# Order of the first maxima, a lead that shrinks, and GpSimd's order of work, in a kernel of FFN, attention and FFN on one Trainium2 core

## The chip, the cores and the metric

The kernel runs on one core of a Trainium2 chip. The time is device microseconds from launch to end, as a median over several executions; the smaller the better. The core's engines run side by side and each takes its own instructions in order: TensorE (PE), VectorE (DVE), ScalarE (ACT), GpSimd (POOL) and SyncE (SP). They wait for one another through semaphores. SP and POOL issue the DMAs that this text speaks of.

## The reference

For one sequence of 2048 tokens with 128 features:

```python
x = x + 0.5 * ffn(layernorm(x))    # 128 -> 512 (ternary weights), gelu, layernorm, 512 -> 128 (ternary weights)
x = x + attention(layernorm(x))    # 16 heads of 8 features
x = x + 0.5 * ffn(layernorm(x))
# attention, per head: q and k are turned by the rotary tables, then
scores = q @ k.T / sqrt(8)         # 2048 x 2048
attn = softmax(scores, axis=-1)
out = attn @ v                     # then all heads together @ wo.T + bo
```

The softmax is taken with the maximum of each row of scores subtracted. The scores are so large that this subtraction is needed, and it has to be the maximum over all 2048 keys.

## The kernel before

There are 8 pairs of heads and 4 chunks of 512 queries, so 32 **groups** (one pair, one chunk of queries; `NG`), taken chunk by chunk. Every group is worked on twice.

**First pass, the maxima.** A group has 16 **max units** (`A_STEP`): 4 key chunks of 512 keys (`kb`) times 4 tiles of 128 queries (`q`). In a unit PE multiplies queries with keys for the two heads of the pair (`max_mm`, L1307, two matmuls of 128x512 into two PSUM banks; there are two such pairs of banks) and DVE takes the maximum over the keys (`row_max`, L819, 128x1024 in, 128x2 out). A max matmul of unit n waits until DVE has done unit n - 2 (`a_free`). There are 512 units in all. One unit after a group's last, DVE joins the four key chunks' maxima (`whole_max`, L827); GpSimd splits the result into three bf16 parts in five small operations (`cut_max`, L526 to L530); two units further on DVE transposes the parts (`max_rows`, L836), for which it waits for GpSimd (`mp_ready`); then SP and POOL send them with four DMAs each (`rows`, L353 and L538) into three extra rows of the queries in `QT`. The second pass's product then gives the score less the maximum, with no further work.

**Second pass, the exponentials.** A group has 16 **exp units**. In one, PE multiplies keys with queries, for the two heads (`exp_mm`, L1326, two matmuls of 128x512, in three PSUM banks in turn), ACT takes the exponential of each (`exp_tile`, L1082), and PE multiplies the result with the values, two units behind (`pv_tile`, L1339, eight matmul records on 128x256). In the third exp of the next group ACT copies the group's sums out of PSUM (`take_out`, L1090), and SP and POOL send them on with four DMAs each (`sums`, L364 and L549).

**The coupling.** PE's list is written out by hand. First come 25 max units (`LEAD`), the last eight of them with a matmul that serves only to keep PE at work (`warm`, L1137). From there on every step holds one exp unit, one max unit that is 25 ahead, and one `pv_tile`. The first exp matmul of a group waits for the group's eight row DMAs (`m_in`). After exp unit 487 there are no max units left; work of the last layers is put among the last exp units (`late`).

**The start of the maxima.** They begin while the keys and queries are still being laid out. For each of the key chunks K0 to K3 and for the first query chunk Q0, DVE and ACT cut the turned values into three bf16 parts (on DVE `rest`, L747, and `last_part`, L754; on ACT `first_cut`, L1009, and `second_cut`, L1015). PE then places them by one-hot matmuls (`place_half`, L1226, six matmuls) and ACT copies them out of PSUM (`put`, L1031 and L1034), in four steps for each: parity 0 or 1 of the pair number, half 0 or 1. Group 0 needs parity 0, group 1 parity 1. In DVE's list the last cuts of K2 and K3 stand behind max units 1, 2, 4 and 5; DVE's last one of K3 waits for ACT's `second_cut("K3")`. PE's list has the placings between the first max units.

**GpSimd's list.** In round i: `sums(i - 1)`, `cut_max(i + 1)`, `rows(i + 1)`, then pieces of the later query chunks. SP has the same order without the cut.

Of the kernel before, what the change touches and what calls it, by code (L numbers as in the profile page):

```python
# [9 lines left out]
ALU = mybir.AluOpType  # L10
# [33 lines left out]
B_STEP = 2 * NT  # L44
QH = CS // 2
PV_LAG = 2
LEAD = 25
PRING = 16
NG = NC * PAIRS
UNITS = NG * A_STEP  # L50
# [4 lines left out]
OUT_AT = 2  # L55
ROW_DMAS = 4
OD_DMAS = 4

WIDE_FROM = (2 * (UNITS - LEAD) + 3) // 4 * 4
WIDE = 5  # L60
# [7 lines left out]

QK_SEQ = ("K0", "Q0", "K1", "K2", "K3")
UNIT_SEQ = ("K0", "Q0", "K1", "Q1", "K2", "Q2", "K3", "Q3")  # L70
PLACE_SEQ = (("K0", 0), ("Q0", 0), ("K1", 0), ("K0", 1), ("Q0", 1), ("K2", 0), ("K1", 1), ("K3", 0), ("K2", 1), ("K3", 1))
UNIT_BANKS = 3
PARTS = 3
VB = 3
# [21 lines left out]
def macaron(nc, x, wq, bq, wk, bk, wv, bv, wo, bo, w_fc, ln_w, ln_b, w_proj, out):  # L96
# [4 lines left out]
    with ExitStack() as ctx:  # L101
# [234 lines left out]
        @block.sync  # L336
        def _(sp):
            tokens = x.rearrange("a (t p) d -> p (a t) d", p=P)
            sp.dma_start(wfc_n[:, :, :], w_fc.rearrange("(k p) d -> p k d", p=P)).then_inc(wf_in, 16)
            sp.dma_start(X[:, 0:CT, :], tokens[:, 0:CT, :]).then_inc(x0_in, 16)  # L340
            sp.dma_start(wpj_n[:, :], w_proj).then_inc(wp_in, 16)
            sp.dma_start(X[:, CT:NT, :], tokens[:, CT:NT, :]).then_inc(x_in, 16)
            sp.wait_ge(x_in, 16)
            sp.wait_ge(w_in, 16 * W_DMAS)
            for n in range(2):
                sp.dma_start(rope[:, n, :], rope_dram[:, n, :]).then_inc(rope_in, 16)

            def rows(g):

                j, c = g % PAIRS, g // PAIRS  # L350
                sp.wait_ge(rows_ready, g + 1)
                for a in range(4):
                    sp.dma_start(row_slots(0, j, c, a), mrow[32 * a:32 * a + 3 * CT, g % 2, :])\  # L353
                        .then_inc(m_in[0][j], 16)

            def sums(g):

                sp.wait_ge(po_free, g + C_ONE + 1)
                if g >= 2 * PAIRS and g % PAIRS == 0:
                    sp.wait_ge(ot_ready, g // PAIRS - 1)  # L360
                for kind in range(2):
                    for half in range(2):
                        to, at = sum_rows(0, kind, half, g)
                        sp.dma_start(to, at).then_inc(o_out[0][g % 2], 16)  # L364

            def spread(c):

                sp.wait_ge(od_rec, c + 1)
                sp.dma_start(recip_dram[c], dense[:, c % 2, :]).then_inc(rec_out, 16)
                sp.wait_ge(rec_out, 16 * (c + 1))  # L370
                whole = recip_dram[c].rearrange("(g s) n -> g (s n)", s=HD)
                sp.dma_start(OD[:, c % 2, 1, :], whole.unsqueeze(1).broadcast_to([NH, HD, CS])).then_inc(rec_in, 16)

            def q_bounce(c):

                sp.wait_ge(q_step, 7 * c)
                sp.dma_start(q_dram[c - 1], q_cut[:, :, :]).then_inc(q_out, 16)

            def q_scatter(c, first):

                sp.wait_ge(q_out, 16 * c)
                for r in range(first, first + Q_DMAS // 2):
                    to, at = q_slots(0, c, r)
                    sp.dma_start(to, at).then_inc(q_in[0][c - 1], 16)

            rows(0)
            for g in range(NG):
                if g:
                    sums(g - 1)
                if g + 1 < NG:  # L390
                    rows(g + 1)
                if g > PAIRS and g % PAIRS == 3:
                    spread(g // PAIRS - 1)
                c = g // Q_STEPS
                if 1 <= c < NC:
                    if g % Q_STEPS == 0:
                        q_bounce(c)
                    else:
                        q_scatter(c, Q_DMAS // 2 * (g % Q_STEPS - 1))
            sums(NG - 1)  # L400

            for c in range(NC):

                sp.wait_ge(y_ready, c + 1)
                sp.dma_start(out.rearrange("a (t p) d -> p (a t) d", p=P)[:, c * CT:(c + 1) * CT, :],
                             chunk(Y, c)).then_inc(y_out, 16)
            sp.wait_ge(y_out, 16 * NC)
# [3 lines left out]
        def _(pool):  # L411
# [149 lines left out]
            for i in range(NG):  # L561
                if i == NG - 1:
                    for c in range(NC - 1):
                        ln_scale(2, c, c)
                if i:
                    sums(i - 1)
                if i + 1 < NG:
                    cut_max(i + 1)
                    rows(i + 1)
                if i > PAIRS and i % PAIRS == 4:  # L570
                    divide(i // PAIRS - 1)
                c = i // Q_STEPS
                if c + 1 < NC:
                    q_piece(c + 1, i % Q_STEPS)
                if 1 <= c < NC and i % Q_STEPS:
                    q_scatter(c, Q_DMAS // 2 * (i % Q_STEPS - 1))
                if i < NC:
                    bias_rows(i)
# [13 lines left out]
        def _(dve):  # L592
# [219 lines left out]

            def row_max(n):

                u = n % A_STEP
                q, kb = u % CT, u // CT
                bank = A0 + 2 * (n % 2)
                dve.wait_ge(a_ready, n + 1)
                v.tensor_reduce(mh[:, n // A_STEP % 2, :, q, kb], ps[:, bank:bank + 2, :], AX.X, ALU.max)\  # L819
                    .then_inc(a_free, 1)  # L820

            def whole_max(i):

                dve.wait_ge(a_free, (i + 1) * A_STEP)
                if i:
                    dve.wait_ge(mp_ready, i)
                v.tensor_reduce(top[:, :], mh[:, i % 2, :, :, :].rearrange("p h q n -> p (h q) n"), AX.X, ALU.max)\  # L827
                    .then_inc(top_ready, 1)
# [17 lines left out]
            for n in range(UNITS):  # L846
# [6 lines left out]
                    rest("K3")  # L853
                if n == 5:
                    last_part("K3")
                g, u = n // A_STEP, n % A_STEP
                if g and u == TOP_AT - 1:
                    whole_max(g - 1)
                if g and u == CUT_AT - 1:
                    max_rows(g - 1)  # L860
                if g > PAIRS and g % PAIRS == 3 and u == REC_AT:
                    reciprocals(g // PAIRS - 1)
            whole_max(NG - 1)
# [45 lines left out]
        def _(act):  # L909
# [152 lines left out]
            put("Q0", 1, 1)  # L1062
            first_cut("K3")
            second_cut("K2")
            put("K2", 0, 0)
            put("K2", 0, 1)
            put("K1", 1, 0)
            put("K1", 1, 1)
            second_cut("K3")
            put("K3", 0, 0)  # L1070
            put("K3", 0, 1)
            put("K2", 1, 0)
# [32 lines left out]
        def _(pe):  # L1105
# [179 lines left out]
            def max_mm(m):  # L1285

                n, x = m // 2, m % 2
                g, u = n // A_STEP, n % A_STEP
                j, c = g % PAIRS, g // PAIRS
                h, q, kb = 1 - x, u % CT, u // CT  # L1290
                rows = slice(HR * h, HR * h + R_QK)
                if x == 0:
                    if n >= 2:
                        pe.wait_ge(a_free, n - 1)
                    elif n == 0:
                        for last in range(2 * len(UNIT_SEQ) - UNIT_BANKS, 2 * len(UNIT_SEQ)):
                            unit_wait(pe, last)
                        pe.wait_ge(v_free, NC)
                    if g == 0 and q == 0:
                        pe.wait_ge(place_ev, 2 * max(PLACE_SEQ.index((y, 0)) for y in ("Q0", f"K{kb}")) + 1)  # L1300
                    if g == 1 and u == 0:
                        pe.wait_ge(place_ev, 2 * len(PLACE_SEQ))
                    if c and j == 0 and u == 0:
                        for part in range(2):
                            pe.wait_ge(q_in[part][c - 1], 16 * Q_DMAS)
                at = c * CS + q * P
# [58 lines left out]
                    last.then_inc(turned, 1)  # L1365


            for n in range(LEAD):
                max_mm(2 * n)
                max_mm(2 * n + 1)  # L1370
                if n == 1:
# [4 lines left out]
                if n == 3:  # L1376
                    place_half("Q0", 1, 1)
                if n == 5:
                    place_half("K2", 0, 0)
                    place_half("K2", 0, 1)  # L1380
                if n == 6:
                    place_half("K1", 1, 0)
                if n == 7:
                    place_half("K1", 1, 1)
                if n == 9:
                    place_half("K3", 0, 0)
                    place_half("K3", 0, 1)
                if n == 10:
                    place_half("K2", 1, 0)
                if n == 11:  # L1390
                    place_half("K2", 1, 1)
                if n == 12:
                    place_half("K3", 1, 0)
                if n == 13:
                    place_half("K3", 1, 1)
                if n > A_STEP:
                    warm(1, EXP[1])
            for g in range(NG):
                for k in range(B_STEP):
                    n = g * B_STEP + k  # L1400
                    exp_mm(g, k)
                    if k % 2 and n + 2 * LEAD < 2 * UNITS:
                        max_mm(n - 1 + 2 * LEAD)
                        max_mm(n + 2 * LEAD)
                    if n < WIDE_FROM:
                        if k % 2 and n // 2 >= PV_LAG:
                            pv_tile(n // 2 - PV_LAG)
# [57 lines left out]
```

## Time and profile before

| | us |
|---|---|
| median of 3 runs | 767.67 (766.25 to 768.15) |
| the profiled execution's own time | 763.32 |
| its span, first to last instruction | 761.4 |
| of that: before the first max unit on DVE | 84.0 |
| first exp matmul on PE | 128.4 |
| last max unit on DVE ends | 688.9 |
| last exponential on ACT ends | 715.9 |

The profile shows one execution. An engine's busy time is the time in which an instruction of it runs; PE's matmuls are pipelined, so a PE that is shown busy need not be at its peak. The times of single instructions are counted from the start of the span. The 2 us between span and time lie outside the instructions.

### The profile page before, as it was taken

The numbers are of one execution on the slowest core, as the hardware profiler recorded it, in microseconds if no ns is written. First come the engines' busy times: TensorE is split into PE (matmuls) and PEld (weight loads), VectorE is DVE, ScalarE is ACT, GpSimd is POOL, SyncE is SP. The second block draws the span as 40 slices with busy tenths as digits, with TensorE's granted clock in tenths as the row PEclk, the third lists the DMA queues.
The fourth block names the chain that finished last, engine by engine and source line by source line (L and its number), as shares of the span: only waits on it lengthen the run. The fifth ranks groups of instructions, "written<-read, shape, count | busy, mean of one in ns | idle before, by whom it ended". The sixth has DMA issues, their size and how long they took to land.

```text
span 761.4 us, 17532 instructions
## 1 busy us (share of the span) xinstructions
PE 722.2 (95%) x6843; PEld 242.9 (32%) x6843; DVE 688.8 (90%) x880; ACT 637.3 (84%) x1196; POOL 256.9 (34%) x526
## 2 busy tenths in 40 slices
PE   5898779999999999999999999999999999999994
PEld 2774211222222222222222222222222222224373
DVE  6678659999999999999999999999999999996374
ACT  3544643999999999999999999999999999999842
POOL 4332001455455445233323332232222222424321
PEclk8999755999999999999999999999999999999998
DMA  7000000000011011011000000000000000000001
GB/s 221 2 1 0 1 0 2 3 5 4 24 25 25 24 25 25 25 24 40 4 4 4 4 4 3 5 19 5 4 4 4 5 6 21 7 7 3 7 15 42
DMA packets 22674, 12.45 MB, mean 16 GB/s; under 512 B 13088, under 2 KB 21152, under 8 KB 22336
## 3 DMA queue, kind: packets, MB, share of 16 engines
q1 hardware_dynamic: 11328, 8.77, 4.1%
q0 software_dynamic: 9056, 2.04, 1.6%
q8 instruction: 54, 0.88, 0.5%
q10 hardware_dynamic: 2208, 0.53, 0.4%
q14 instruction: 28, 0.23, 0.1%
HBM read 7.34 MB, written 2.33 MB: 13 GB/s over the span
## 4 chain that ended last, share of the span: by engine, by line
DVE 63%; PE 28%; issue 4%; ACT 2%; DMA 1%; POOL 0%; SPq 0%; DVEq 0%; POOLq 0%; ACTq 0%
DVE mh L819 59%; PE ps L1339 7%; PE ps L1326 5%; PE ps L1126 3%; PE ps L1307 3%; PE ps L1226 2%; PE ps L1185 2%; PE ps L1202 2%; ACT KT L1031 1%; DVE ring L681 1%; PE ps L1354 1%; DMA X<-in_L_attn_x_dram 1%; DMA QT<-mrow 0%; PE ps L1192 0%; DVE mrow L836 0%
## 5 line engine op out<-in xcount | busy, mean ns | idle before, releaser
L819 DVE TENSOR_REDUCE mh<-ps 128x2 f32<-128x1024 f32 x512 | 584.8, 1213 | 6.3 <-PE ps L1307 6.2
L1082 ACT ACTIVATE ring<-ps 128x512 f32<-128x512 f32 x1024 | 551.2, 600 | 30.6 <-PE ps L1326 15.9
L1339 PE MATMUL ps<-ring,Vx 128*32 128x256 f32 x4096 | 325.4, 392 | 0.9 <-ACT outT L1090 0.9
L1307 PE MATMUL ps<-KT,QT 48*128 48x512 bf16 x1024 | 209.3, 392 | 10.1 <-DVE mh L819 9.7
L1326 PE MATMUL ps<-QT,KT 51*128 51x512 bf16 x1024 | 212.6, 388 | 1.7 <-DMA QT<-mrow 0.6
L1339 PEld LDWEIGHTS ps<-ring,Vx 128*32 128x32 f32 x4096 | 82.0, 108 | 172.0 <-ACT ring L1082 156.4
L1326 PEld LDWEIGHTS ps<-QT,KT 51*128 51x128 bf16 x1024 | 51.9, 93 | 220.6 <-ACT ring L1082 205.6
L549 POOL DMA_DIRECT2D rope<-outT x80 | 42.9, 542 | 147.4 <-ACT outT L1090 139.6
L538 POOL DMA_DIRECT2D QT<-mrow x128 | 71.7, 565 | 42.2 <-DVE mrow L836 38.7
L526 POOL TENSOR_TENSOR mp<-zeros,top 128x8 bf16<-128x8 f32 x32 | 6.3, 198 | 223.3 <-DVE top L827 223.3
L1307 PEld LDWEIGHTS ps<-KT,QT 48*128 48x128 bf16 x1024 | 50.1, 94 | 52.4 <-DVE mh L819 23.8
L959 ACT ACTIVATE ring<-ps 128x512 f32<-128x512 f32 x32 | 18.0, 601 | 26.2 <-PE ps L1126 14.3
L1126 PE MATMUL ps<-QT,WfcT 128*128 128x512 f32 x64 | 32.8, 651 | 2.0 <-ACT QT L946 1.4
L1185 PE MATMUL ps<-WpC,ring 128*128 128x129 f32 x256 | 30.4, 276 | 1.5 <-ACT ring L959 1.5
L1185 PEld LDWEIGHTS ps<-WpC,ring 128*128 128x128 f32 x256 | 29.4, 191 | 2.5 <-ACT ring L959 1.6
L1031 ACT ACTIVATE KT<-ps,k_ones 128x1024 bf16<-128x1024 f32 x16 | 17.4, 1111 | 14.4 <-PE ps L1226 14.3
L549 POOL DMA_DIRECT2D dense<-outT x48 | 24.0, 505 | 1.0 <-issue 0.9
L681 DVE TENSOR_TENSOR ring<-ring 128x512 f32<-128x512 f32 x24 | 18.8, 784 | 1.2
L1090 ACT COPY outT<-ps 128x256 f32<-128x256 f32 x32 | 12.0, 374 | 9.3 <-PE ps L1339 9.3
L457 POOL TENSOR_TENSOR rsh<-var,half_neg 128x4 f32<-128x4 f32 x8 | 9.3, 1161 | 28.5 <-DVE var L703 28.5
L965 ACT ACTIVATE ring<-ring 128x512 f32<-128x512 f32 x32 | 17.6, 636 | 0.0
L1202 PE MATMUL ps<-ring,WQK 128*128 128x512 f32 x32 | 17.3, 661 | 0.1
(133 smaller groups left out, 344.0 us busy)
## 6 DMA issues: line engine op xcount, KB each, us to landing
rope<-rope_tables SPq DMA_DIRECT2D x2, 1024.0 KB, 6.2
QT<-mrow SPq DMA_DIRECT2D x128, 0.8 KB
QT<-mrow POOLq DMA_DIRECT2D x128, 0.8 KB, 1.7
rope<-outT SPq DMA_DIRECT2D x80, 8.0 KB
rope<-outT POOLq DMA_DIRECT2D x80, 8.0 KB, 1.7
q_bounce<-XB SPq DMA_DIRECT2D x3, 384.0 KB, 2.4
QT<-q_bounce SPq DMA_DIRECT2D x18, 64.0 KB
QT<-q_bounce POOLq DMA_DIRECT2D x18, 64.0 KB, 3.2
```

The lines of the kernel that those rows point to most:

```text
L538: g.dma_start(row_slots(1, j, c, a), mrow[32 * a + 3 * CT:32 * a + 6 * CT, i % 2, :])\
L549: g.dma_start(to, at).then_inc(o_out[1][i % 2], 16)
L681: last = v.tensor_tensor(sqsum[:, n % 2, :], sqsum[:, n % 2, :] if k > 1 else sq[:, 0, :], sq[:, k, :], ALU.add)
L819: v.tensor_reduce(mh[:, n // A_STEP % 2, :, q, kb], ps[:, bank:bank + 2, :], AX.X, ALU.max)\
L1031: a.activation(KT[:, first:first + 3:2, c * CS:(c + 1) * CS], at, ACT.Identity, bias=k_ones[:, 3:4])\
L1082: a.activation(ring[:, n % PRING, :], ps[:, exp_bank(n), :], ACT.Exp, scale=SCALE).then_inc(p_ready, 1)
L1126: t.matmul(ps[:, FC + k, :], WfcT[:, k * P:(k + 1) * P], XF[:, c * CS:(c + 1) * CS], start=True, stop=True).then_inc(fc_ready, 1)
L1185: last = t.matmul(out_tile(i, n % 2)[:, 0:D + 1], hid[:, k, i * P:(i + 1) * P], WpC[:, k, :], start=(k == 0), stop=(k == KH - 1))
L1202: t.matmul(ps[:, u % UNIT_BANKS, :], WQK[:, n, k, :], XT[:, c % 2, :], start=True, stop=True)\
L1307: mm = t.matmul(ps[:, A0 + 2 * (n % 2) + h, :], QT[rows, j, at:at + P], KT[rows, j, kb * CS:(kb + 1) * CS], start=True, stop=True)
L1326: t.matmul(ps[:, exp_bank(n), :], KT[rows, j, kt * P:(kt + 1) * P], QT[rows, j, c * CS:(c + 1) * CS], start=True, stop=True).then_inc(b_re ...
L1339: mm = t.matmul(ps[r:r + 32, PO, 0:QH], Vx[:, kt, col:col + 32], ring[:, (2 * n + h) % PRING, half * QH:(half + 1) * QH], start=(kt == 0), ...
```

## The change

1. **Order of the maxima.** The 32 max units of groups 0 and 1 are done together, by key chunk: chunk 0 of both groups, chunk 1 of both, chunks 2 and 3 of group 0, chunks 2 and 3 of group 1 (`TURNS`, `ORDER`). Group 0 then ends with unit 23 instead of 15, group 1 with unit 31 as before (`LAST_OF`); `whole_max` and `max_rows` follow one and three units behind. The waits for the placings are per key chunk in group 1 too.
2. **Order of the placings.** K1's parity 1 comes before K2's parity 0 in PE's and ACT's lists, ACT's `second_cut("K3")` comes two `put`s earlier, and no two halves are placed right behind each other from K1 parity 1 on.
3. **Lead.** 34 max units stand ahead of the first exp unit instead of 25 (six of them with a `warm` instead of eight). At exp units 47, 95, ..., 431 the max unit is left out, so that the lead falls by one each time, to 25.
4. **GpSimd's and SP's order.** In rounds 0 to 10 `cut_max(i + 1)` and `rows(i + 1)` stand ahead of `sums(i - 1)`; from round 11 on as before.

```diff
+LEAD_FIRST = 34
 LEAD = 25
+LEAD_STEP = 48
+CUTS_FIRST = 11
...
+TURNS = ((0, 0), (1, 0), (0, 1), (1, 1), (0, 2), (0, 3), (1, 2), (1, 3))
+ORDER = [(g, q, kb) for g, kb in TURNS for q in range(CT)]
+ORDER += [(g, u % CT, u // CT) for g in range(2, NG) for u in range(A_STEP)]
+LAST_OF = [max(n for n, (of, _, _) in enumerate(ORDER) if of == g) for g in range(NG)]
...
-PLACE_SEQ = (("K0", 0), ("Q0", 0), ("K1", 0), ("K0", 1), ("Q0", 1), ("K2", 0), ("K1", 1), ("K3", 0), ("K2", 1), ("K3", 1))
+PLACE_SEQ = (("K0", 0), ("Q0", 0), ("K1", 0), ("K0", 1), ("Q0", 1), ("K1", 1), ("K2", 0), ("K3", 0), ("K2", 1), ("K3", 1))
...
             for g in range(NG):
+                if g < CUTS_FIRST:
+                    rows(g + 1)
                 if g:
                     sums(g - 1)
-                if g + 1 < NG:
+                if CUTS_FIRST <= g < NG - 1:
                     rows(g + 1)
...
+                if i < CUTS_FIRST:
+                    cut_max(i + 1)
+                    rows(i + 1)
                 if i:
                     sums(i - 1)
-                if i + 1 < NG:
+                if CUTS_FIRST <= i < NG - 1:
                     cut_max(i + 1)
                     rows(i + 1)
...
+                if n - TOP_AT in LAST_OF:
+                    whole_max(LAST_OF.index(n - TOP_AT))
+                if n - CUT_AT in LAST_OF:
+                    max_rows(LAST_OF.index(n - CUT_AT))
                 g, u = n // A_STEP, n % A_STEP
-                if g and u == TOP_AT - 1:
-                    whole_max(g - 1)
-                if g and u == CUT_AT - 1:
-                    max_rows(g - 1)
...
             second_cut("K2")
-            put("K2", 0, 0)
-            put("K2", 0, 1)
             put("K1", 1, 0)
             put("K1", 1, 1)
             second_cut("K3")
+            put("K2", 0, 0)
+            put("K2", 0, 1)
...
-                    if g == 0 and q == 0:
-                        pe.wait_ge(place_ev, 2 * max(PLACE_SEQ.index((y, 0)) for y in ("Q0", f"K{kb}")) + 1)
-                    if g == 1 and u == 0:
+                    if g < 2 and q == 0:
+                        pe.wait_ge(place_ev, 2 * max(PLACE_SEQ.index((y, g)) for y in ("Q0", f"K{kb}")) + 1)
+                    if g == 2 and q == 0 and kb == 0:
                         pe.wait_ge(place_ev, 2 * len(PLACE_SEQ))
...
-            for n in range(LEAD):
+            for n in range(LEAD_FIRST):
                 max_mm(2 * n)
                 max_mm(2 * n + 1)
...
                 if n == 5:
+                    place_half("K1", 1, 0)
+                if n == 6:
+                    place_half("K1", 1, 1)
+                if n == 8:
                     place_half("K2", 0, 0)
+                if n == 9:
                     place_half("K2", 0, 1)
-                if n == 6:
-                    place_half("K1", 1, 0)
-                if n == 7:
-                    place_half("K1", 1, 1)
-                if n == 9:
+                if n == 11:
                     place_half("K3", 0, 0)
+                if n == 12:
                     place_half("K3", 0, 1)
-                if n == 10:
+                if n == 14:
                     place_half("K2", 1, 0)
-                if n == 11:
+                if n == 15:
                     place_half("K2", 1, 1)
-                if n == 12:
+                if n == 17:
                     place_half("K3", 1, 0)
-                if n == 13:
+                if n == 18:
                     place_half("K3", 1, 1)
-                if n > A_STEP:
+                if n > 27:
                     warm(1, EXP[1])
+            lead = LEAD_FIRST
             for g in range(NG):
                 for k in range(B_STEP):
                     n = g * B_STEP + k
                     exp_mm(g, k)
-                    if k % 2 and n + 2 * LEAD < 2 * UNITS:
-                        max_mm(n - 1 + 2 * LEAD)
-                        max_mm(n + 2 * LEAD)
+                    if k % 2 and lead > LEAD and n // 2 % LEAD_STEP == LEAD_STEP - 1:
+                        lead -= 1
+                    elif k % 2 and n + 2 * lead < 2 * UNITS:
+                        max_mm(n - 1 + 2 * lead)
+                        max_mm(n + 2 * lead)
```

## Rows read from the trace of the kernel before

**Rows 1.** Chain that ended last, shares by line.
```profile
DVE mh L819 59%; PE ps L1339 7%; PE ps L1326 5%; PE ps L1126 3%; PE ps L1307 3%; PE ps L1226 2%; PE ps L1185 2%; PE ps L1202 2%; ACT KT L1031 1%; DVE ring L681 1%; PE ps L1354 1%; DMA X<-in_L_attn_x_dram 1%; DMA QT<-mrow 0%; PE ps L1192 0%; DVE mrow L836 0%
```
**Rows 2.** Stretches: busy us and instructions of PE, PEld, DVE, ACT, POOL; clock; DMA.
```profile
205.03:223.32 18.29, 18.26 (x194) 5.10 (x192) 18.29 (x20) 17.54 (x34) 9.53 (x18) 1.00 0.12 25
...
131.20:134.60 3.40, 3.40 (x24) 0.54 (x22) 2.80 (x3) 1.94 (x4) 0.00 (x0) 0.50 0.00 0
134.60:138.00 3.40, 3.40 (x42) 0.89 (x40) 3.08 (x4) 2.93 (x6) 0.00 (x0) 1.00 0.02 5
```
**Rows 3.** Timeline of ACT, copies of groups' sums: start, us, instruction, idle before.
```profile
150.25 0.37 ACT L1090 COPY outT<-ps 128x256 f32<-128x256 f32 x1 [0.22 <-PE ps L1339]
...
186.75 0.37 ACT L1090 COPY outT<-ps 128x256 f32<-128x256 f32 x1 [0.24 <-PE ps L1339]
205.03 0.37 ACT L1090 COPY outT<-ps 128x256 f32<-128x256 f32 x1 [0.24 <-PE ps L1339]
...
627.19 0.37 ACT L1090 COPY outT<-ps 128x256 f32<-128x256 f32 x1 [0.24 <-PE ps L1339]
```
**Rows 4.** Timeline of DVE, 14 max units of a group in a row.
```profile
142.26 15.89 DVE L819 TENSOR_REDUCE mh<-ps 128x2 f32<-128x1024 f32 x14
```
**Rows 5.** Timeline of PE, exp pairs from 336 to 355 us, behind a stall.
```profile
336.54 0.39 PE L1326 MATMUL ps<-QT,KT 51*128 51x512 bf16 x2
...
353.19 0.81 PE L1326 MATMUL ps<-QT,KT 51*128 51x512 bf16 x2
354.72 0.39 PE L1326 MATMUL ps<-QT,KT 51*128 51x512 bf16 x2
```
**Rows 6.** Timeline of DVE and of PE, what lengthened single groups.
```profile
311.31 0.54 DVE L844 RECIPROCAL dense<-dense 128x64 f32<-128x64 f32 x1
...
331.66 0.39 PE L1326 MATMUL ps<-QT,KT 51*128 51x512 bf16 x2 [0.57 <-DMA QT<-mrow]
```
**Rows 7.** Timeline of PE, the last step with a max unit and the first without.
```profile
686.79 0.39 PE L1326 MATMUL ps<-QT,KT 51*128 51x512 bf16 x2
...
687.89 0.39 PE L1326 MATMUL ps<-QT,KT 51*128 51x512 bf16 x2
...
688.79 1.06 PE L1326 MATMUL ps<-QT,KT 51*128 51x512 bf16 x4
```
**Rows 8.** Timeline of DVE, last cut of K3, max units 19 to 27, 29 to 32.
```profile
102.61 0.69 DVE L754 TENSOR_TENSOR XB<-X,XB 128x512 bf16<-128x512 f32 x1 [5.59 <-ACT XB L1015]
...
122.66 10.44 DVE L819 TENSOR_REDUCE mh<-ps 128x2 f32<-128x1024 f32 x9
...
135.25 4.62 DVE L819 TENSOR_REDUCE mh<-ps 128x2 f32<-128x1024 f32 x4 [0.33 <-PE ps L1307]
```
**Rows 9.** Timeline of ACT, copies of placed keys and the second cut of K3.
```profile
96.26 2.12 ACT L1031 ACTIVATE KT<-ps,k_ones 128x1024 bf16<-128x1024 f32 x2 [3.96 <-PE ps L1226]
...
101.97 0.61 ACT L1015 CAST XB<-X 128x512 bf16<-128x512 f32 x1
```
**Rows 10.** Timeline of PE, placings, and the first exp units.
```profile
94.76 1.48 PE L1226 MATMUL ps<-early,place 32*128 32x512 bf16 x12
...
97.52 1.46 PE L1226 MATMUL ps<-XB,place 32*128 32x512 bf16 x6 [0.74 <-ACT KT L1031]
...
127.29 0.61 PE L1307 MATMUL ps<-KT,QT 48*128 48x512 bf16 x2
...
128.37 0.61 PE L1326 MATMUL ps<-QT,KT 51*128 51x512 bf16 x2
...
132.62 0.61 PE L1326 MATMUL ps<-QT,KT 51*128 51x512 bf16 x2
...
134.60 0.39 PE L1326 MATMUL ps<-QT,KT 51*128 51x512 bf16 x2
```
**Rows 11.** Timeline of POOL, the sums' DMAs and the cut of one group.
```profile
187.41 1.07 POOL L549 DMA_DIRECT2D rope<-outT  x2 [1.21 <-ACT outT L1090]
...
194.89 0.20 POOL L526 TENSOR_TENSOR mp<-zeros,top 128x8 bf16<-128x8 f32 x1 [5.41 <-DVE top L827]
```

More of the change, by code:

```diff
@@ L813, in row_max @@
             def row_max(n):
-                u = n % A_STEP
-                q, kb = u % CT, u // CT
+                g, q, kb = ORDER[n]
                 bank = A0 + 2 * (n % 2)
                 dve.wait_ge(a_ready, n + 1)
-                v.tensor_reduce(mh[:, n // A_STEP % 2, :, q, kb], ps[:, bank:bank + 2, :], AX.X, ALU.max)\
+                v.tensor_reduce(mh[:, g % 2, :, q, kb], ps[:, bank:bank + 2, :], AX.X, ALU.max)\
                     .then_inc(a_free, 1)
             def whole_max(i):
-                dve.wait_ge(a_free, (i + 1) * A_STEP)
+                dve.wait_ge(a_free, LAST_OF[i] + 1)
                 if i:
@@ L1287, in max_mm @@
                 n, x = m // 2, m % 2
-                g, u = n // A_STEP, n % A_STEP
+                g, q, kb = ORDER[n]
                 j, c = g % PAIRS, g // PAIRS
-                h, q, kb = 1 - x, u % CT, u // CT
+                h = 1 - x
                 rows = slice(HR * h, HR * h + R_QK)
@@ L1298, in max_mm @@
                         pe.wait_ge(v_free, NC)
-                    if g == 0 and q == 0:
-                        pe.wait_ge(place_ev, 2 * max(PLACE_SEQ.index((y, 0)) for y in ("Q0", f"K{kb}")) + 1)
-                    if g == 1 and u == 0:
+                    if g < 2 and q == 0:
+                        pe.wait_ge(place_ev, 2 * max(PLACE_SEQ.index((y, g)) for y in ("Q0", f"K{kb}")) + 1)
+                    if g == 2 and q == 0 and kb == 0:
                         pe.wait_ge(place_ev, 2 * len(PLACE_SEQ))
-                    if c and j == 0 and u == 0:
+                    if c and j == 0 and q == 0 and kb == 0:
                         for part in range(2):
```

## The prediction

> **What bounds the kernel now.** I read the chain of waits first: DVE's maxima are 59% of it, PE's value and exp matmuls 12% [rows 1]. The table of stretches comes next. In one group of the steady middle DVE is busy for 18.29 of 18.29 us, PE for 18.26, ACT for 17.54 at overlapping instructions, and the clock is 1.00 [rows 2]. So two engines could be the bound, and which one it is decides the change. The timelines tell them apart.
>
> DVE: 14 max units take 15.89 us, so one starts every (15.89 - 1.22) / 13 = 1.13 us; 16 of them and 0.2 for a group's top and transpose are 18.28, which is the distance of two copies of sums, 186.75 to 205.03 [rows 3, 4]. DVE paces that group. PE: behind a stall it runs free for a whole group. Its exp pairs go from 336.54 to 354.72, 18.18 us for 16 steps; 15 steps are 1.11 and one, at the group's seam, 353.19 to 354.72, is 1.53, since ACT copies the sums there [rows 5]. So PE needs 18.18 a group and DVE 18.28: **PE is only 0.10 us a group away from being the bound itself.** ACT isn't one: its step is that of PE in both cases, with room in PE's waits at the seam alone.
>
> The sum is made against the profiled execution: 763.32 us, of which 761.4 are the span. The median of the runs is 767.67, 4.3 above it; I add the difference that I find to the median.
>
> **Part 1 and 2: the first 34 max units.** Before, DVE stood idle 5.59 us ahead of the last cut of K3 [rows 8], since ACT reached its second cut of K3 only at 101.97, behind four `put`s, two of which waited for placings [rows 9]. In the new order two of them remain ahead of it. K1's parity 1 is placed at 94.76 (a half takes 1.46 busy and 1.41 to the next, from 97.52 [rows 10]), the second half behind the next max pair at 96.7, its copy ends at 99.3, the cut of K3 follows and ends at 99.9. DVE's last cut starts there, 2.7 us before 102.61. Nothing ahead of it moves: max unit 4 is of group 1 now and needs Q0's parity 1, whose copy stands ahead of all this on ACT.
>
> From there I walked the two lists. DVE needs 1.13 for a unit. PE needs, at the low clock, 0.54 for a max pair (127.29 to 127.83 is one, then a filler of the same length up to the exp pair at 128.37 [rows 10]) and 1.41 for a placing, so 1.95 for a unit that has one. Eight units from 8 to 18 have one, where before two placings, those of K2 and K3 at parity 0, ran as a pair: 12 matmuls in 1.48 [rows 10]. With three units to 0.54 x 3 + 1.41 x 2 = 4.4 PE against 3.4 on DVE, DVE is short by about 1 us per three units while placings last. Unit 6 starts at 100.5, unit 9 at 104.4, unit 12 at 108.8, unit 15 at 113.2, unit 18 at 117.6, unit 19 at 119.6. Unit 19 started at 122.66 before [rows 8]. So the order gains **3.1 us** on DVE at unit 19, of which 2.7 is the cut. Then DVE runs on without a gap, where before it was PE with its fillers that set 1.15 a unit (10.44 for nine) and the slow first exp units: unit 31 ends at 119.6 + 12 x 1.13 + 0.3 (top and transpose of group 0) + 1.2 less the overlap of 0.1 = 134.6, and unit 32 ends at 135.7 against 139.87 before (135.25 + 4.62 [rows 8]): 4.2 us earlier.
>
> The Trainium skill has a rule that speaks against this part: in "TensorE: Matmul & The Clock Gate", section "Why this matters for your kernels", matmuls of few rows that use distinct groups of rows run at the same time. By it the two halves of a placing, which use different rows, cost one half's time when they stand together, and the new order, which pulls K2's and K3's apart, pays 2 x 1.41 = 2.8 us more on PE; priced by the count of matmuls it would pay nothing. The trace agrees with the rule (12 in 1.48 beside 6 in 1.46 [rows 10]).
>
> **Part 3: the lead.** The first exp pair comes behind 34 max units. The last of these is issued when DVE has done unit 31, at 134.6; a pair and a filler later (1.08, as 127.29 to 128.37) the exp pair starts at 135.7. Before it was 128.37 [rows 10]. **The exponentials start 7.3 us later.** Group 0's rows are no hindrance: its transpose is at about 128.7, 7.0 ahead of the exp pair, where before there were 5.8. What the exp units then save:
> - A step without a max pair takes 0.90 (687.89 to 688.79) instead of 1.10 (686.79 to 687.89) [rows 7]. Nine of them save 9 x 0.2 = 1.8.
> - With 47 max units to 48 exp units DVE needs 3 x 18.28 - 1.13 = 53.7, PE 3 x 18.18 - 0.2 = 54.3. So PE becomes the bound and DVE gets idle time of 0.6 in every step of the lead. From the first sums' copy to that of group 26 there were 26 groups in 627.19 - 150.25 = 476.9 [rows 3]. At PE's pace they are 26 x 18.18 = 472.7, less 1.8: 470.9. That saves **6.0 us**. It contains three stalls of 0.4, where DVE's reciprocals (0.54, the first at 311.31) broke its pace, and one of 0.57, where an exp pair waited for rows behind other DMAs at 331.66 [rows 6]; an idle DVE and earlier rows hide them.
> - After exp unit 432 the lead is 25 again, and everything to the end is as before.
>
> The sum: 7.3 - 6.0 = **+1.3 us**. The 6.2 us from the first exp pair to the high clock (128.37 to 134.60 [rows 2, 10]) are taken to be as long as before. The profiled execution would be 764.6, the median 769.0.
>
> Bounds: PE's pace can't be above DVE's 18.28 without being the old kernel's; were it 18.28 in free running too, 2.6 of the 6.0 would be gone: +3.9. If PE could be left out and DVE alone set the end, the 4.2 us of max unit 32 are the other bound: -4.2.
>
> **Part 4: GpSimd's order.** With a lead of 34 the top of group i + 1 comes at exp unit 16i or so, two units before the sums' copy. The five operations (0.20 each from 194.89, 0.28 apart) take 1.3, the four DMAs of sums 2 x 1.07 [rows 11]. Behind these, the parts would be late by about 3 us and DVE's transpose would wait; the new order avoids that, so it costs nothing and gains nothing against before, where the top came seven units behind. What is queued behind the two waits on POOL (for the top, for the transpose) are the sums' DMAs, the pieces of later queries and, on SP, its own sums: up to 5 us later, while the copy that needs their buffer is a group off. In round 11, with lead 31, the cut stands behind the sums again, with 2.2 us until the transpose; it can be late by 0.3, which DVE's new idle time takes up. If that cover is gone it is 0.3, once.
>
> **The rivals.**
> - *DVE is the bound all the way.* Then the end follows DVE: 4.2 earlier, less what DVE loses in the slow first exp units as before (0.60 in 131.20 to 134.60, 0.32 in the next 3.4 us [rows 2]), so -3.3: 764.4. For it: DVE is the engine that is busy for the full 18.29 and has 59% of the chain. Against it: PE's free group of 18.18.
> - *The clock stays low longer, and the kernel gets slower.* Its place is the start of the exp units. A step takes 1.98 (132.62 to 134.60) at clock 0.50 and 1.11 after it [rows 2, 5, 10], so each us more at the low clock costs 0.44. PE is less dense than before from 119.6 to 129, since the fillers there are gone. With 3.2 us more the price is 1.4: +2.6, 770.3. It decides from 2.5 us more on. Against it: before, too, the clock stayed low throughout the fillers and rose only when value matmuls ran.
> - *The cut of K3 is not earlier*, because the halves of K1 wait or PE holds ACT up. Then the change doesn't do what part 2 says; the exponentials start 2.7 later still: +3.9, 771.6.
>
> **How the numbers follow.** From no change this kernel's measurement can tell about 0.3%, 2.3 us. Forecast +1.3: 0.50, its own range -1.0 to +3.5, of which same 0.39, slower 0.10, faster 0.01. DVE bound: 0.22, of which faster 0.19, same 0.03. Low clock: 0.15, slower 0.09, same 0.06. Late cut: 0.13, slower 0.11, same 0.02. Together faster 0.20, same 0.50, slower 0.30. The range goes from DVE's bound, less 0.5 (763.9), to late cut plus some of the low clock (+4.6, 772.3).
>
> **What would show it.** DVE's last cut of K3 at 99.9 and max unit 32 ending near 135.7; the first exp pair at 135.7; sums' copies 18.1 apart (three groups 54.3) up to group 26 and 18.28 after it; DVE idle by 0.2 a group, waiting for max matmuls; no wait for rows. It is wrong if the copies stay at 18.28 while the lead falls (then +3.9), if DVE has no idle time but groups are shorter than 18.1, or if the first exp pair is off by more than 1.5 us.

## The result and the profile after

The changed kernel is **slower: ratio 1.0048, 95% interval 1.0038 to 1.0058**. Its median is 768.53 us (767.79 to 771.97, 20 runs) against 764.98 us (763.30 to 768.15, 20 runs) for the kernel before, so +3.6 us. The forecast was +1.3, with 0.50 for "no change" and 0.30 for "slower"; the time lies in the range, the move lies outside what I called no change (2.3 us). That the forecast time, 769.0, and the measured 768.53 agree within 0.5 us is luck: the forecast stood on a median of 767.67 over three runs of the kernel before, and over 20 runs it is 764.98.

The two profiled executions differ by more, 770.26 and 763.32, because the first is high and the second low in what its kernel scatters. So I compare stretches that start at an event of the kernel: the first max unit on DVE, the first exp pair on PE, the copies of the sums on ACT.

| us | before | before, second profile | after | after with cut order 14 |
|---|---|---|---|---|
| first max unit to max unit 19 | 38.65 | 37.79 | 33.86 | 35.11 |
| first max unit to first exp pair | 44.36 | 43.50 | 49.98 | 51.23 |
| first exp pair to first copy of sums | 21.89 | 22.75 | 22.88 | 21.89 |
| first copy to copy of group 26 | 476.94 | 477.00 | 474.57 | 473.95 |
| copy of group 26 to copy of group 31 | 90.75 | 90.75 | 90.60 | 90.60 |
| copy of group 31 to the end | 43.45 | 45.08 | 45.09 | 43.45 |

(The second and the fourth column are experiments told below; the fourth is the same code as the third up to round 11. The start of the exp units and the stretches at the low clock scatter by 1 to 2 us from execution to execution, so two profiles of each are shown.) Between the means of two columns each: the exp units start 6.7 later, the 26 groups give back 2.7 (2.4 in the changed kernel itself), the rest 0.15. That is +3.8 to +4.1, beside +3.6 measured.

The chain of waits has moved from DVE to PE (shares of the span by line; L832 is the maximum, L1352 the values, L1339 the exp pairs, L1320 the max pairs). Beside it stands [rows 1].

```profile
PE 78%; DVE 15%; issue 3%; ACT 2%; POOL 1%; DMA 1%; DVEq 0%; POOLq 0%; SPq 0%; ACTq 0%
PE ps L1352 32%; PE ps L1339 20%; PE ps L1320 13%; DVE mh L832 11%; PE ps L1139 3%; PE ps L1198 2%; PE ps L1239 2%; PE ps L1215 1%; ACT KT L1044 1%; DVE ring L695 1%; PE ps L1367 1%; DMA X<-in_L_attn_x_dram 1%; PE ps L1205 0%; PE ps L1225 0%; DVE X L727 0%
```

The timeline of ACT after, the copies of the sums (start, us, instruction, idle before), beside [rows 3]. Groups are 18.18 apart where they were 18.28; 176.39 to 194.53, which holds a step without a max pair, is 18.14, only 0.04 less; and 340.26 to 359.11 is 18.85.

```profile
158.21 0.37 ACT L1103 COPY outT<-ps 128x256 f32<-128x256 f32 x1 [0.22 <-PE ps L1352]
176.39 0.37 ACT L1103 COPY outT<-ps 128x256 f32<-128x256 f32 x1 [0.22 <-PE ps L1352]
194.53 0.37 ACT L1103 COPY outT<-ps 128x256 f32<-128x256 f32 x1 [0.22 <-PE ps L1352]
212.71 0.37 ACT L1103 COPY outT<-ps 128x256 f32<-128x256 f32 x1 [0.22 <-PE ps L1352]
...
340.26 0.37 ACT L1103 COPY outT<-ps 128x256 f32<-128x256 f32 x1 [0.24 <-PE ps L1352]
359.11 0.37 ACT L1103 COPY outT<-ps 128x256 f32<-128x256 f32 x1 [0.22 <-PE ps L1352]
...
632.78 0.37 ACT L1103 COPY outT<-ps 128x256 f32<-128x256 f32 x1 [0.22 <-PE ps L1352]
```

The table of stretches after (busy us and instructions of PE, PEld, DVE, ACT, POOL; clock; DMA), beside [rows 2]: a group without a short step, and the last stretch at the low clock with the next one.

```profile
212.71:230.89 18.18, 18.15 (x194) 4.61 (x192) 18.18 (x19) 17.54 (x33) 9.53 (x18) 1.00 0.16 26
140.40:143.82 3.42, 3.42 (x24) 0.67 (x24) 2.41 (x2) 1.98 (x4) 3.42 (x3) 0.50 0.03 6
143.82:147.24 3.42, 3.42 (x40) 0.82 (x36) 2.97 (x4) 3.11 (x6) 0.18 (x1) 1.00 0.00 0
```

The timeline of DVE after, the first maxima, beside [rows 8]. The last cut of K3 (L768) starts at 99.92, and DVE then waits 0.71 for a max pair at every third unit.

```profile
99.92 0.69 DVE L768 TENSOR_TENSOR XB<-X,XB 128x512 bf16<-128x512 f32 x1 [2.82 <-ACT XB L1028]
...
114.91 3.59 DVE L832 TENSOR_REDUCE mh<-ps 128x2 f32<-128x1024 f32 x3 [0.71 <-PE ps L1320]
119.20 6.88 DVE L832 TENSOR_REDUCE mh<-ps 128x2 f32<-128x1024 f32 x6 [0.71 <-PE ps L1320]
```

The timeline of PE after, a step without a max pair (a **short step**; it starts at 191.11), beside [rows 7]. It takes 0.89. The next takes 1.29. All nine such places show these two numbers. DVE then waits for its max pair (third fence; the second has the two ACT exponentials that the reading of the banks below rests on).

```profile
191.11 0.39 PE L1339 MATMUL ps<-QT,KT 51*128 51x512 bf16 x2
...
192.00 0.57 PE L1339 MATMUL ps<-QT,KT 51*128 51x512 bf16 x2
...
193.29 0.39 PE L1339 MATMUL ps<-QT,KT 51*128 51x512 bf16 x2
...
194.40 0.39 PE L1339 MATMUL ps<-QT,KT 51*128 51x512 bf16 x2
```
```profile
190.42 0.60 ACT L1095 ACTIVATE ring<-ps 128x512 f32<-128x512 f32 x1
...
191.53 0.60 ACT L1095 ACTIVATE ring<-ps 128x512 f32<-128x512 f32 x1
```
```profile
192.83 2.36 DVE L832 TENSOR_REDUCE mh<-ps 128x2 f32<-128x1024 f32 x2 [0.47 <-PE ps L1320]
```

### The profile page after: what moved, and what is told of

Same layout as the page of the kernel before. It is cut to its first block, busy times and chain, and to the rows that moved or that the text cites. A ratio compares the mean times of both kernels' runs of the same rounds, so it can differ in the third digit from the quotient of the medians.

```text
span 768.5 us, 17532 instructions
## 1 busy us (share of the span) xinstructions
PE 729.2 (95%) x6841; PEld 243.1 (32%) x6841; DVE 690.6 (90%) x880; ACT 636.4 (83%) x1196; POOL 256.9 (33%) x526
## 4 chain that ended last, share of the span: by engine, by line
PE 78%; DVE 15%; issue 3%; ACT 2%; POOL 1%; DMA 1%; DVEq 0%; POOLq 0%; SPq 0%; ACTq 0%
PE ps L1352 32%; PE ps L1339 20%; PE ps L1320 13%; DVE mh L832 11%; PE ps L1139 3%; PE ps L1198 2%; PE ps L1239 2%; PE ps L1215 1%; ACT KT L1044 1%; DVE ring L695 1%; PE ps L1367 1%; DMA X<-in_L_attn_x_dram 1%; PE ps L1205 0%; PE ps L1225 0%; DVE X L727 0%
## 5 line engine op out<-in xcount | busy, mean ns | idle before, releaser
L832 DVE TENSOR_REDUCE mh<-ps 128x2 f32<-128x1024 f32 x512 | 586.2, 1211 | 12.0 <-PE ps L1320 11.9
L1352 PE MATMUL ps<-ring,Vx 128*32 128x256 f32 x4096 | 325.9, 392 | 0.9 <-ACT outT L1103 0.9
L1320 PE MATMUL ps<-KT,QT 48*128 48x512 bf16 x1024 | 211.4, 395 | 12.6 <-DVE mh L832 12.4
L1339 PE MATMUL ps<-QT,KT 51*128 51x512 bf16 x1024 | 214.8, 389 | 1.1
L1352 PEld LDWEIGHTS ps<-ring,Vx 128*32 128x32 f32 x4096 | 82.3, 108 | 187.7 <-ACT ring L1095 167.0
L1339 PEld LDWEIGHTS ps<-QT,KT 51*128 51x128 bf16 x1024 | 52.9, 93 | 221.0 <-ACT ring L1095 205.7
L1320 PEld LDWEIGHTS ps<-KT,QT 48*128 48x128 bf16 x1024 | 50.3, 95 | 44.5 <-DVE mh L832 29.7
L1198 PE MATMUL ps<-WpC,ring 128*128 128x129 f32 x256 | 33.6, 294 | 1.5 <-ACT ring L972 1.5
L1198 PEld LDWEIGHTS ps<-WpC,ring 128*128 128x128 f32 x256 | 32.6, 209 | 2.5 <-ACT ring L972 1.6
L457 POOL TENSOR_TENSOR ve<-mv,eps 128x4 f32<-128x4 f32 x12 | 3.2, 264 | 41.6 <-DVE mv L617 41.6
```

Source lines behind the costliest of these rows:

```text
L832: v.tensor_reduce(mh[:, g % 2, :, q, kb], ps[:, bank:bank + 2, :], AX.X, ALU.max)\
L1198: last = t.matmul(out_tile(i, n % 2)[:, 0:D + 1], hid[:, k, i * P:(i + 1) * P], WpC[:, k, :], start=(k == 0), stop=(k == KH - 1))
L1320: mm = t.matmul(ps[:, A0 + 2 * (n % 2) + h, :], QT[rows, j, at:at + P], KT[rows, j, kb * CS:(kb + 1) * CS], start=True, stop=True)
L1339: t.matmul(ps[:, exp_bank(n), :], KT[rows, j, kt * P:(kt + 1) * P], QT[rows, j, c * CS:(c + 1) * CS], start=True, stop=True).then_inc(b_re ...
L1352: mm = t.matmul(ps[r:r + 32, PO, 0:QH], Vx[:, kt, col:col + 32], ring[:, (2 * n + h) % PRING, half * QH:(half + 1) * QH], start=(kt == 0), ...
```

## The experiments

The theory: a unit of lead costs one DVE step at the start; in return, while the lead falls, a group takes 18.18 instead of 18.28 us. The rivals: the orders of maxima and placings are what costs; or PE's own work sets the 18.18, and then a step without a max pair is worth 0.2 us (called P in the expectations); or the loop between PE and ACT over three exp banks sets it, and such a step is worth nothing (L).

**The lead alone.** The orders of the changed kernel are set back:

```diff
-TURNS = ((0, 0), (1, 0), (0, 1), (1, 1), (0, 2), (0, 3), (1, 2), (1, 3))
+TURNS = ((0, 0), (0, 1), (0, 2), (0, 3), (1, 0), (1, 1), (1, 2), (1, 3))
...  (PLACE_SEQ, ACT's puts and PE's placings as in the kernel before)
```

> Parts 3 and 4 without parts 1 and 2: orders of maxima and placings as before, first lead 34, nine steps down to 25, GpSimd's order as changed. The first exp pair comes nine DVE steps later than before, 44.4 + 10.3 = 54.7 us behind the first max unit; the groups then save 2.4 us between the first sums' copy and that of group 26, as in the changed kernel. In all +7.5 to +8 us on the kernel before, 1.010; the orders are then worth 4 to 4.5 us of the changed kernel. Rival: the orders themselves are what costs (placings pulled apart), so that this kernel is no slower than the changed one, 1.005.

Ratio 1.0106 (1.0084 to 1.0128, median 774.15). The first exp pair comes 54.07 behind the first max unit (54.7 expected), and the 26 groups take 474.61, as expected. The rival falls: the orders are worth 1.0106 - 1.0048, some 4.4 us of gain (by the two intervals, 2.6 to 6.3), and the lead costs more than they bring.

**A lead of 31.**

```diff
-LEAD_FIRST = 34
+LEAD_FIRST = 31
...
-                    if g == 2 and q == 0 and kb == 0:
+                    if g == 1 and q == 0 and kb == 3:
                         pe.wait_ge(place_ev, 2 * len(PLACE_SEQ))
```

> The changed kernel with a first lead of 31 instead of 34 (six steps down to 25 instead of nine). Both theories price a unit of lead at the start at 1.13 us (DVE's step), so the first exp pair comes 3.4 us earlier than with 34. Theory L (a loop over the three exp banks sets 1.108 us a step, a step without a max pair saves nothing): nine groups fewer run at 18.18 instead of 18.28, +0.9, so -2.5 against the changed kernel, about 1.0015 of the kernel before. Theory P (PE's own work sets the step, each step without a max pair saves 0.2): +1.5, so -1.9, 1.0023 of the kernel before. If the first group's rows come too late for it, the first exp pair waits for a DMA and the gain is under 1.5.

Ratio 1.0031 (1.0017 to 1.0044), so 0.0017 or 1.3 us less than with 34, at the edge of what the two intervals tell apart. By its middle the gain is smaller than both theories said and fits the third case of the expectation. The timeline of PE shows why: the first exp pair waits for the first group's rows.

```profile
133.18 0.61 PE L1339 MATMUL ps<-QT,KT 51*128 51x512 bf16 x2 [0.80 <-DMA QT<-mrow]
```

It stands 48.74 behind the first max unit, against 49.98 and 51.23 with 34. Since group 0 ends at unit 23 and its rows are already awaited here, I take it that a lead under 31 would start the exp units no earlier in this order; no run shows it, and the new orders with the old lead of 25 were not run either. The 26 groups take 474.41, no more than the 474.57 of lead 34. The nine further groups at 18.18 bought nothing, because their 0.9 stands against two things: the wait in round 11 (below) is missing here, and one of DVE's reciprocals began 1.0 us ahead of a short step and was taken up by it (18.18 for its group; with lead 34 it began 4.8 us ahead, and its group took 18.58). L and P are not told apart by this run.

**Half of the value matmuls' columns.** This kernel leaves most keys out of half of the sums and divides the exponent by 64; its output is not the reference's.

```diff
-                        mm = t.matmul(ps[r:r + 32, PO, 0:QH], Vx[:, kt, col:col + 32],
-                                      ring[:, (2 * n + h) % PRING, half * QH:(half + 1) * QH],
+                        part = QH if kt == 0 else QH // 2
+                        mm = t.matmul(ps[r:r + 32, PO, 0:part], Vx[:, kt, col:col + 32],
+                                      ring[:, (2 * n + h) % PRING, half * QH:half * QH + part],
...  (and scale=SCALE / 64 in ACT's exponential)
```

> The changed kernel with the value matmuls at half their columns (128 instead of 256) for all key tiles but the first of a group, so that half of the sums leave out most keys, and with the exponent divided by 64, so that no sum becomes zero; all other work, all waits and all sizes of ACT and DVE stay. It takes some 0.25 us of PE's work out of each step. Theory P: PE is no bound any more, steps behind a seam take under 1.0 us and three groups take DVE's 53.7 us instead of 54.5, in all at least 7 us less. Theory L: steps behind a seam stay at 1.10 to 1.11 us and three groups at 54.2 to 54.5; under 3 us less between the first copy of sums and that of group 26.

The timeline of ACT of this kernel: 272.13 to 290.42 is 18.29, then 17.83, and with the 17.89 from 254.24 three groups take 54.0.

```profile
254.24 0.37 ACT L1103 COPY outT<-ps 128x256 f32<-128x256 f32 x1
272.13 0.37 ACT L1103 COPY outT<-ps 128x256 f32<-128x256 f32 x1 [0.24 <-PE ps L1353]
290.42 0.37 ACT L1103 COPY outT<-ps 128x256 f32<-128x256 f32 x1 [0.25 <-PE ps L1353]
308.25 0.37 ACT L1103 COPY outT<-ps 128x256 f32<-128x256 f32 x1
```

Of three groups one is DVE's 18.28 again, and the two around the short step are 0.4 shorter each. DVE sets them: in these three groups it waits 0.2 us, once. Behind the seam (the step in which ACT copies the sums) that follows a short step, two or three steps take 0.98 or 0.99 us, where L said 1.10 to 1.11, and three groups take less than L's 54.2. L falls, and PE's work is what holds a full group at 18.18. P's size isn't reached either: 54.0 instead of 53.7, and the 26 groups take 470.5, 4.1 less than 474.57, where P said 7 and L under 3; 0.8 of the difference was lost in the first of them (18.96), which began at the low clock.

PE's timeline at a short step of this kernel: the step is 0.21 shorter than in the changed kernel (0.68), and the next takes 1.29 all the same, as its second exp matmul waits 0.4 us for ACT. PE's weight loads (PEld) and ACT show that wait:

```profile
197.24 0.39 PE L1339 MATMUL ps<-QT,KT 51*128 51x512 bf16 x2
...
197.92 0.78 PE L1339 MATMUL ps<-QT,KT 51*128 51x512 bf16 x2
...
199.21 0.47 PE L1339 MATMUL ps<-QT,KT 51*128 51x512 bf16 x2
```
```profile
197.67 0.60 ACT L1095 ACTIVATE ring<-ps 128x512 f32<-128x512 f32 x1
```
```profile
198.31 0.09 PEld L1339 LDWEIGHTS ps<-QT,KT 51*128 51x128 bf16 x1 [0.30 <-ACT ring L1095]
```

The time of the whole tells nothing (ratio 1.000, 0.9975 to 1.0025): in the profiled execution the clock stayed at 1.2 GHz until 167.6, and the first copy came 27.7 behind the first exp pair instead of 22.9. Two of the other executions took 760 us, at a mean granted clock of 0.95 instead of the 0.94 of this one (766.65).

**Sums first in all rounds (part 4 undone).**

```diff
-CUTS_FIRST = 11
+CUTS_FIRST = 0
```

> The changed kernel with part 4 undone (the sums' DMAs ahead of the cut in all rounds, on POOL and SP). The cut has to wait for the sums' copy, which comes about two steps after the top while the lead is 34, then for four DMAs (2.1 us): DVE's transpose waits about 3 us a group at first and less as the lead falls, and the whole falls behind by 15 to 30 us. Rival: DVE's lead over ACT takes it up, and the time stays within 2 us of the changed kernel.

Ratio 1.0523 (1.0499 to 1.0547), 804.76. The 26 groups take 511.18, 36.6 more; copies are up to 24.7 apart. DVE and POOL at one group: the sums' DMAs, then the cut, and DVE's transpose behind it.

```profile
207.21 1.07 POOL L560 DMA_DIRECT2D rope<-outT  x2 [13.37 <-ACT outT L1103]
208.27 1.00 POOL L560 DMA_DIRECT2D dense<-outT  x2
209.28 0.22 POOL L537 TENSOR_TENSOR mp<-zeros,top 128x8 bf16<-128x8 f32 x1
```
```profile
210.65 0.21 DVE L849 STREAM_TRANSPOSE mrow<-mp 128x32 bf16<-128x32 bf16 x1 [3.44 <-POOL mp L541]
```

DVE waits for the cut in 11 groups, 4.3 us in the first two, 3.4 in the third, which the fences show, and less as the lead falls, down to 0.6: 26.3 us in all. That is about what was expected and the rival (within 2 us) falls; that the whole lost more than 30 us was not. A DVE that stands still lets PE run dry, and the clock fell to 1.2 GHz six times between 162 and 306 us. The first of them (PE's wait, then the stretch, columns as above):

```profile
163.04 0.61 PE L1320 MATMUL ps<-KT,QT 48*128 48x512 bf16 x2 [3.70 <-DVE mh L832]
```
```profile
162.30:169.10 6.80, 6.06 (x38) 1.10 (x38) 5.40 (x5) 2.17 (x4) 5.82 (x7) 0.50 0.02 1
```

How the 10 us beyond DVE's waits divide between the low clock and PE's refilling was not measured.

**GpSimd's order up to round 13.**

```diff
-CUTS_FIRST = 11
+CUTS_FIRST = 14
```

> The changed kernel with GpSimd's new order up to round 13 instead of 10. In round 11 the sums stood ahead of the cut and DVE's transpose waited 0.58 us for it; this wait goes, and the distance of the sums' copies of groups 10 and 11 falls from 18.85 to 18.2, with nothing given back later: 0.6 us less between the first copy and that of group 26 (474.0). Rival: the lost time comes from the query chunk's DMAs in the same round, and the distance stays.

One execution, as expected. In the changed kernel DVE's transpose of round 11 waits for the cut (first fence, the timeline of DVE after); here copies of groups 10 and 11 are 18.18 apart (second fence), and the 26 groups take 473.95, 0.62 less.

```profile
344.38 0.21 DVE L849 STREAM_TRANSPOSE mrow<-mp 128x32 bf16<-128x32 bf16 x1 [0.58 <-POOL mp L541]
```
```profile
339.75 0.37 ACT L1103 COPY outT<-ps 128x256 f32<-128x256 f32 x1 [0.25 <-PE ps L1352]
357.93 0.37 ACT L1103 COPY outT<-ps 128x256 f32<-128x256 f32 x1 [0.22 <-PE ps L1352]
```

**The kernel before once more.**

> The kernel before once more, unchanged, for a second profile of it. The groups keep 18.28 and the first exp pair stays 44.4 us behind the first max unit; the start of the first max unit (84.0 in the first profile, 84.4 to 85.4 in five others) and the stretches at the low clock near the end vary from execution to execution. Rival: the first max unit always starts at 84.0 in this kernel, and the later start belongs to the change.

One execution. The first max unit starts at 85.28, the groups take 18.28, and the first exp pair comes 43.5 behind the first max unit (0.9 less than expected). The late start of the maxima belongs to neither kernel.

```profile
85.28 2.36 DVE L819 TENSOR_REDUCE mh<-ps 128x2 f32<-128x1024 f32 x2 [0.97 <-PE ps L1307]
```

**The early cut of K3, in the kernel before.** In the changed kernel the gain at the start came with the lead's cost. This asks for the gain alone.

```diff
             second_cut("K2")
+            second_cut("K3")
             put("K2", 0, 0)
             put("K2", 0, 1)
             put("K1", 1, 0)
             put("K1", 1, 1)
-            second_cut("K3")
```

> The kernel before with one line moved: ACT's second cut of K3 ahead of the four copies of K2 and K1, all else as before. DVE's last cut of K3 starts at about 97 instead of 102.6; PE's placings then pace units 6 to 13 at 1.95 us each, so unit 14 starts at about 112 instead of 116.8 and the first exp pair at about 123.5 instead of 128.4. As DVE paces the groups at 18.28 from there, the whole gain stays: -4.5 to -5 us, about 0.994 of the kernel before. Rival: placings take it all back, and nothing is gained; or the later copies of K2 cost as much.

**Ratio 0.9958** (0.9942 to 0.9974, median 761.72). The first exp pair stands 40.19 behind the first max unit (44.36 and 43.50 before), the groups are unchanged (476.90). The gain of 3.3 to 4.2 stays to the end (-3.2 in the medians), somewhat under the 4.5 expected, and both rivals fall.

```profile
125.31 0.60 PE L1326 MATMUL ps<-QT,KT 51*128 51x512 bf16 x2
```

**Early cut, and both halves of each placing together.**

```diff
                 if n == 2:
                     place_half("Q0", 1, 0)
-                if n == 3:
                     place_half("Q0", 1, 1)
...
                 if n == 6:
                     place_half("K1", 1, 0)
-                if n == 7:
                     place_half("K1", 1, 1)
...  (K2 parity 1 at 11, K3 parity 1 at 13, both halves together)
```

> The kernel before with the early cut of K3 and with the two halves of every placing issued right behind each other (12 matmuls in 1.5 us instead of twice 1.4), so that PE has about 4 us less to do while it paces the maxima. From the cut of K3 on, DVE (1.13 a unit) and ACT's ten copies (1.0 to 1.1 each) set the pace: unit 17 starts about 3 us earlier than with the early cut alone, and the first exp pair about 37 us behind the first max unit instead of 40.2. In all -6 to -7.5 us on the kernel before, 0.991. Rival: the copies on ACT take the place of PE's placings and less than 1 us is gained over the early cut alone.

**Ratio 0.9921** (0.9902 to 0.9940, median 759.77): this version beats both kernels. Its median is 5.7 us under that of the kernel before (6 to 7.5 expected). The first exp pair stands 37.64 behind the first max unit, 2.6 less than with the early cut alone, so the rival (under 1 us) falls. The timeline of PE of this kernel: where ACT has copied both halves' banks, 12 matmuls take 1.48; where the second half still waits for a copy, 2.47.

```profile
103.28 1.48 PE L1226 MATMUL ps<-XB,place 32*128 32x512 bf16 x12
...
106.03 2.47 PE L1226 MATMUL ps<-early,place 32*128 32x512 bf16 x12 [0.31 <-ACT KT L1031]
...
123.44 0.61 PE L1326 MATMUL ps<-QT,KT 51*128 51x512 bf16 x2
```

## Why the prediction was right, and where it wasn't

The bound was read rightly and the time lies in the range, but +3.6 lies at the upper edge of the range of the forecast itself (-1.0 to +3.5). What the whole range had above that was for a late cut and a low clock, and neither was what cost the time. So the range held for another reason than the one it was made for: the exp units gave back 3.3 to 3.6 less than forecast, and a start that was 0.6 to 1.7 better than forecast made up for a part of it.

**Which engine bounds a group: right.** PE's free group of 18.18 was read from one group behind a stall [rows 5], and with a falling lead the groups took 18.18. The chain went over to PE. DVE's idle time for want of a max pair between the copies rose from 0.3 to 5.6 us, in 16 waits. It isn't spread over all groups as I wrote: in a group at the whole lead DVE is busy for 18.18 of 18.18, it falls behind by 0.1 a group, and it idles behind the short steps. The rival "DVE all the way" fails by this.

**The first 34 units: right, and one exact hit is luck.** K3's last cut started at 99.92, forecast 99.9, but the first max unit of that execution started 1.3 us later than in the profile that the forecast was worked out from. Counted from the first max unit, the cut came 14.6 to 15.9 us after it in the five profiles with the new order and 18.6 and 17.7 in the two of the kernel before: 2.7 earlier in the means, as forecast. Max unit 32 ended at 135.32 (forecast 135.7), 4.6 to 5.9 earlier by the same count (forecast 4.2). The gain at unit 19, from the first max unit, is 2.7 to 4.8 us over the four profiles (forecast 3.1); "the cut is not earlier" fails. The walk put a gap of about 1 us into three units; it was 0.71.

**The start of the exp units: nearly right.** Forecast +7.3; from the first max unit it is +5.6 in the changed kernel's profile against the first profile of before, +6.7 over the means.

**What the exp units give back: this step failed**, forecast 6.0, measured 2.4. By its terms:
- *26 groups at 0.10 less, 2.6:* came.
- *Nine steps without a max pair, "0.90 instead of 1.10", 1.8:* nearly nothing came. The step took 0.89, but the next 1.29, 2.18 for both against 2.22. Where nothing else fell into a group with such a step, it took 18.14 or 18.15 (four groups) and later 18.17 or 18.18 (three), against 18.18 for a group without. I had the 0.20 from 687.89 [rows 7], where the next pair was followed by another kind of step and five exp banks are in use. In the lead there are three, so PE can only be 1.5 units ahead of ACT: behind the short step the second exp matmul waits for its bank (192.00, 0.57 long for two that take 0.39), and the max pair and the values are queued behind it in PE's order. ACT's exponential on that bank, three exp matmuls back, ends at 192.13 and the matmul starts at 192.18. With half of the value columns it is the same at 198.27 and 198.32: there the step behind the short one has 0.21 less work on PE too and still takes 1.29, so the wait took up the difference. In a full step that bank is free only 0.09 us ahead of the matmul (191.02 and 191.11), so by an estimate from these rows a step on its own can be shorter by some 0.04 before the wait sets in. No run with more banks was made.
- *Three reciprocals hidden, 1.2:* nearly all of it was not. The groups with one took 18.44, 18.58 and 18.63, so 1.1 of the 1.2 stayed. DVE has no idle time except behind the short steps, so 0.54 more on it goes through unless such a step follows at once, as with lead 31.
- *The wait for rows hidden, 0.6:* came (18.28 for 18.88), and the cut in round 11 took the same amount: 0.58 of waiting, 18.85 for the group.

The sum with what was measured is 6.7 - 2.4 - 0.15 = +4.1, beside +3.6 in the medians.

**Part 4: the cover was right, and the price of round 11 wasn't.** Without the new order the cut is 4.3 us late at first and less from group to group (forecast about 3). Round 11 was put at 0.3 and as taken up by DVE's idle time; it was 0.58 and nothing took it up, for the same reason as the reciprocals.

**The low clock.** It lasted 8.5 us from the first exp pair instead of 6.2 in the two profiles [rows 2]; in the two further profiles it was 8.1 before and 6.2 after. So both kernels show both lengths, and the rival that makes the change slower by it isn't borne out.

## What to carry to other kernels

A lead that has to be built before the second pass starts costs one step of the slower engine per unit, and buys only the difference between the two engines' paces while it is used up; here a unit cost 1.1 us and bought some 0.3 (three groups at 0.10). When an order frees the first pass, take the gain with the lead as it is, as the two versions with the early cut did. And the price of a step that is made shorter has to be read where the same buffers are in use: with three banks a short step was given back in the next one.

## What the runs showed of the hardware that I had not expected

- The clock can drop for 3.4 us in the last layers of either kernel (the table of stretches after, columns as above). From the last copy of sums to the end it takes 45.08 or 45.09 with such a stretch (four of the ten profiles) and 43.45 without; it was absent from the first profile of before and present in the second. PE's work ahead of it doesn't tell the two apart: in the 3.5 us before this place PE is busy for 2.19 us in the changed kernel and in the first profile of before, and for 2.18 in the second.

```profile
744.60:748.00 3.40, 3.40 (x17) 3.40 (x18) 1.78 (x10) 1.70 (x4) 1.02 (x1) 0.50 0.00 0
```

- With half of the value columns the clock stayed at 1.2 GHz for some 24 us longer (to 167.6 instead of 143.8) in the profiled execution, though PE is shown busy throughout from 150 to 160. The first copy came 4.8 us later for it, which is more than the 4.1 that the groups gained.
- The two halves of a placing, on different rows, ran at the same time only where nothing stood between them: 1.48 for both, 1.39 or 1.40 each with a max pair between. Putting them together moved the first exp pair by 2.6 us, and with the early cut by 6.
